# Finer first loads of Wq and later loads of bq and bk in a two-sublayer kernel (cross attention and quantised FFN)

## The reference

```python
def _L0_xattn_ref(text, features, Wq, bq, Wk, bk):
    Q = jnp.einsum('btx,dx->btd', text, Wq) + bq
    K = jnp.einsum('bpx,dx->bpd', features, Wk) + bk
    scores = jnp.einsum('btd,bpd->btp', Q, K) * scale
    attn = jax.nn.softmax(scores, axis=-1)
    return jnp.einsum('btp,bpd->btd', attn, features)

x = x + _L0_xattn_ref(_layernorm(x), ctx_4096, Wq, bq, Wk, bk)
x = x + _L0_ffn_ref(_layernorm(x), qweight, qzeros, scales, bias, g_idx)
```

## Time and profile before

| | before |
|---|---|
| median of three runs | 555.83 us |
| the profiled execution, its own time | 556.69 us |
| its span | 554.9 us |
| TensorE matmul busy | 546.3 us (98%) |
| VectorE busy | 385.4 us (69%) |
| ScalarE busy | 239.1 us (43%) |
| GpSimd busy | 186.1 us (34%) |
| first stage's share of the DMA: 0 to 16 us | 200 to 420 GB/s, engines nearly always busy |

### The profile page before, as it was taken

How to read it: one execution, slowest core, us unless ns; L and a number is a source line. 1 busy time by engine, 2 the same in 40 slices (tenths; PEclk the granted TensorE clock), 3 DMA queues, 4 the chain that set the end, 5 groups by cost and what they waited for, 6 DMA issues and landing times.

```text
span 554.9 us, 7445 instructions
## 1 busy us (share of the span) xinstructions
PE 546.3 (98%) x2702; PEld 456.5 (82%) x2702; DVE 385.4 (69%) x643; ACT 239.1 (43%) x426; POOL 186.1 (34%) x143
## 2 busy tenths in 40 slices
PE   7999999999999999999999999999999999999997
PEld 5888888887777877878889999999788888888886
DVE  4987776689889997784213555574877788778742
ACT  5964354301431341242427666676473253234210
POOL 2072000000000000000125977776667545743630
PEclk9999999999999999999999999999999999999999
DMA  8842100349677745743345699897517776773411
GB/s 270 275 156 73 38 1 0 112 160 314 207 205 262 220 190 175 220 168 143 130 138 203 250 350 351 318 402 301 229 77 227 229 219 235 214 241 108 123 76 76
DMA packets 47187, 106.59 MB, mean 192 GB/s; under 512 B 3576, under 2 KB 24064, under 8 KB 44976
## 3 DMA queue, kind: packets, MB, share of 16 engines
q1 hardware_dynamic: 40624, 99.84, 51.2%
q10 hardware_dynamic: 6528, 6.29, 5.2%
HBM read 66.27 MB, written 39.85 MB: 191 GB/s over the span
## 4 chain that ended last, share of the span: by engine, by line
PE 86%; DVE 5%; ACT 4%; DMA 2%; issue 2%; POOL 1%; SPq 0%; ACTq 0%; DVEq 0%; POOLq 0%
PE bank L1235 22%; PE bank L1237 22%; PE bank L1236 22%; PE bank L1279 5%; PE bank L1282 5%; PE bank L1285 5%; PE bank L1337 2%; DMA wk_stage<-in_L_xattn_Wk 1%; DMA right_scratch<-part_hi 1%; ACT yin L789 1%; POOL cn_lo L537 1%; PE bank L1245 1%; ACT cn_hi L586 1%; PE bank L1320 1%; DVE junk L1001 0%
## 5 line engine op out<-in xcount | busy, mean ns | idle before, releaser
L1235 PE MATMUL bank<-xT_hi,m_hi 128*128 128x512 f32 x256 | 103.4, 404 | 0.4 <-DVE xT_lo L853 0.4
L1236 PE MATMUL bank<-xT_lo,m_hi 128*128 128x512 f32 x256 | 99.7, 389 | 0.0
L1237 PE MATMUL bank<-xT_hi,m_lo 128*128 128x512 f32 x256 | 99.7, 389 | 0.0
L745 ACT ACTIVATE t_pair<-bank,ucol 128x512 f32<-128x512 f32 x32 | 22.0, 686 | 107.0 <-PE bank L1237 107.0
L544 POOL TENSOR_TENSOR tT_lo<-t_pair,tT_hi 128x1024 fp32r<-128x1024 f32 x16 | 38.2, 2405 | 75.0 <-ACT tT_hi L586 75.0
L1187 DVE TENSOR_TENSOR xres<-xres,bank 128x512 f32<-128x512 f32 x56 | 38.1, 681 | 36.2 <-PE bank L1237 36.1
L523 POOL TENSOR_TENSOR pairs<-mv,pairs 128x2 f32<-128x2 f32 x8 | 5.5, 692 | 161.3 <-DVE mv L920 161.3
L558 POOL TENSOR_TENSOR l_lo_s<-l_sum_s,l_hi_s 128x512 fp32r<-128x512 f32 x32 | 40.4, 1298 | 56.0 <-DVE l_sum_s L1128 56.0
L1235 PEld LDWEIGHTS bank<-xT_hi,m_hi 128*128 128x128 f32 x256 | 48.1, 188 | 12.3 <-DVE xT_lo L853 0.8
L1237 PEld LDWEIGHTS bank<-xT_hi,m_lo 128*128 128x128 f32 x256 | 48.0, 188 | 10.1
L1236 PEld LDWEIGHTS bank<-xT_lo,m_hi 128*128 128x128 f32 x256 | 48.1, 188 | 9.9 <-issue 0.2
(11 more groups left out here) (148 smaller groups left out, 1255.7 us busy)
## 6 DMA issues: line engine op xcount, KB each, us to landing
cin<-in_ctx SPq DMA_DIRECT2D x8, 1024.0 KB, 5.7
xres<-in_x SPq DMA_DIRECT2D x8, 1024.0 KB, 11.2
out<-xres SPq DMA_DIRECT2D x15, 512.0 KB, 5.7
right_scratch<-part_hi SPq DMA_DIRECT2D x28, 256.0 KB, 2.2
xn_scratch<-xin SPq DMA_DIRECT2D x6, 1024.0 KB, 4.9
xq<-xn_scratch ACTq DMA_DIRECT2D x24, 256.0 KB, 5.6
r_tile<-right_scratch SPq DMA_DIRECT2D x6, 1024.0 KB, 11.3
yn_scratch<-yin SPq DMA_DIRECT2D x6, 1024.0 KB, 4.4
```

The costliest lines, as they stand in the source:

```text
L745: act.activation(t_pair[p][:, :, j, :], bank[n % 4][:, :].rearrange("p (b q) -> p b q", b=2), ACT.Identity, bias=ucol[:, j:j + 1]).then_in ...
L1235: pe.matmul(out_, a_hi, b_hi, start=start, stop=False, skip_group_check=True)
L1236: pe.matmul(out_, a_hi, b_lo, start=False, stop=False, skip_group_check=True)
L1237: return pe.matmul(out_, a_lo, b_hi, start=False, stop=stop, skip_group_check=True)
```

## The change

Three edits, all in the first stage.

1. The first load of each of Wq's blocks 0 and 1 carries two K tiles (128 KB) and no longer four (256 KB). The K tiles 2 and 3 of both blocks are loaded behind slice 1 of Wk; tiles 4 to 7 stay where they were, behind slice 2. ScalarE and VectorE split the first two tiles alone (`first_split`), and tiles 2 and 3 in front of slice 2's split; TensorE waits for them at c = 2.
2. bq and bk are loaded behind slice 4 of Wk, where they stood in front of slice 2.
3. `times_bq` and `add_u` run two slices later: `times_bq(c - 4)` behind the split of slice c. Four of them are left for behind the loop, where two were.

```diff
+            def first_wq(b, lo, hi, done):
+                sp.dma_start(wq_stage[b][:, lo:hi, :], wq_rows[:, lo:hi, b * P:(b + 1) * P]).then_inc(done, 16)
-            first_wq(0, 0, s_wq0[0])
+            first_wq(0, 0, 2, s_wq00[0])
             for h, done in enumerate((s_wk0, s_wkl[0])):
                 cols = slice(h * HALF, (h + 1) * HALF)
                 sp.dma_start(wk_stage[0][:, cols], wk_rows[:, 0, cols]).then_inc(done, 16)
-            first_wq(1, 0, s_wq0[1])
+            first_wq(1, 0, 2, s_wq00[1])
             for c in range(1, NB):
                 if c == 2:
-                    for r, row in enumerate((bq, bk)):
-                        sp.dma_start(bcols[:, r, :], row.rearrange("(p c) -> p c", c=NB)).then_inc(s_small, 16)
+                    for b in range(2):
+                        first_wq(b, 2, KH, s_wq0[b])
                 if c == 3:
                     for b in range(2):
-                        first_wq(b, 1, s_wql[b])
+                        first_wq(b, KH, NB, s_wql[b])
...
                 sp.dma_start(wk_stage[c % N_STAGE], wk_rows[:, c, :]).then_inc(s_wkl[c % N_STAGE], 16)
+                if c == 4:
+                    for r, row in enumerate((bq, bk)):
+                        sp.dma_start(bcols[:, r, :], row.rearrange("(p c) -> p c", c=NB)).then_inc(s_small, 16)
...
         @block.scalar
+            def first_split(b):
+                act.wait_ge(s_wq00[b], 16)
+                copy(wq_hi[b][:, 0:2, :], wq_stage[b][:, 0:2, :]).then_inc(s_wqhi0, 1)
+
             def wq_split(b, h):
-                cs = slice(KH * h, KH * (h + 1))
+                cs = slice(2 if b < 2 and h == 0 else KH * h, KH * (h + 1))
...
+                if c == 2:
+                    wq_split(0, 0)
+                    wq_split(1, 0)
...
-                if c > 1:
-                    times_bq(c - 2)
-            times_bq(NB - 2)
-            times_bq(NB - 1)
+                if c > 3:
+                    times_bq(c - 4)
+            for c in range(NB - 4, NB):
+                times_bq(c)
...
         @block.vector
+            def first_split(b):
+                dve.wait_ge(s_wqhi0, b + 1)
+                low(wq_lo[b][:, 0:2, :], wq_stage[b][:, 0:2, :], wq_hi[b][:, 0:2, :], s_wqlo0)
...
-                if c > 2:
-                    add_u(c - 2)
-            add_u(NB - 2)
-            add_u(NB - 1)
+                if c > 4:
+                    add_u(c - 4)
+            for c in range(NB - 4, NB):
+                add_u(c)
...
         @block.tensor
+                if first:
+                    pe.wait_ge(s_wqhi0, 1)
+                    pe.wait_ge(s_wkhi, 1)
+                elif b == 1 and c == 0:
+                    pe.wait_ge(s_wqlo0, 2)
+                elif c == KH or c == (2 if b < 2 else 0):
+                    pe.wait_ge(s_wqlo, wq_split_count(b, c // KH))
```

More of the change, by code:

```diff
@@ L194, in xattn_ffn_kernel @@
         s_wk0 = sem("half_of_first_wk_slice_loaded")
+        s_wq00 = [sem(f"first_of_wq_block{i}_loaded") for i in range(2)]
         s_wq0 = [sem(f"half_of_wq_block{i}_loaded") for i in range(2)]
+        s_wqhi0, s_wqlo0 = sem("first_of_wq_hi"), sem("first_of_wq_lo")
         s_wkl = [sem(f"wk_loaded{i}") for i in range(N_STAGE)]
@@ L319, in load_wq @@
                 sp.dma_start(wq_stage[b % 3], wq_rows[:, :, b * P:(b + 1) * P]).then_inc(s_wql[b % 3], 16)
-            def first_wq(b, h, done):
-                cs = slice(KH * h, KH * (h + 1))
-                sp.dma_start(wq_stage[b][:, cs, :], wq_rows[:, cs, b * P:(b + 1) * P]).then_inc(done, 16)
-            first_wq(0, 0, s_wq0[0])
+            def first_wq(b, lo, hi, done):
+                sp.dma_start(wq_stage[b][:, lo:hi, :], wq_rows[:, lo:hi, b * P:(b + 1) * P]).then_inc(done, 16)
+            first_wq(0, 0, 2, s_wq00[0])
             for h, done in enumerate((s_wk0, s_wkl[0])):
@@ L611, in times_bk @@
                 ins.then_inc(s_wqbk, 1)
-            wq_split(0, 0)
+            first_split(0)
             for h, loaded in enumerate((s_wk0, s_wkl[0])):
@@ L617, in _ @@
                 copy(wk_hi[:, 0, cols], wk_stage[0][:, cols]).then_inc(s_wkhi, 1)
-            wq_split(1, 0)
+            first_split(1)
             for c in range(1, NB):
+                if c == 2:
+                    wq_split(0, 0)
+                    wq_split(1, 0)
                 if c == 3:
@@ L1283, in proj @@
                     if first:
-                        pe.wait_ge(s_wqlo, 1)
+                        pe.wait_ge(s_wqlo0, 1)
                     ins = pe.matmul(out_, q_lo, wk_hi[:, c, cols], start=False, stop=c == NB - 1, skip_group_check=True)
```

## The result

| | before | changed |
|---|---|---|
| median of six runs | 555.74 us | 559.57 us |
| lowest and highest | 555.34, 557.14 | 558.86, 559.94 |
| ratio of the changed kernel to the one before | | 1.0063, 95% interval 1.0052 to 1.0074 |
| span of the profiled execution | 554.9 us | 557.7 us |

The prediction was 555.4 us with a range of 554.4 to 556.6. The changed kernel is 3.5 us slower by the ratio (555.74 x 0.0063), and 3.8 us by the medians.

A forecast was written before the change was run, and what follows sets the result against it. TensorE was taken as the bound from end to end: 0.85 us gained at c = 1, 0.4 lost again in front of block 3, so 555.83 - 0.4 = 555.4 us, range 554.4 to 556.6.

The forecast's parts named there:

- Slice 1 was to land at 8.1: First stage's start: halved first loads bring Wk's slice 1 in 0.85 us earlier, 0.3 to 1.05.
- two more loads don't delay slice 2: Loads behind slice 1: slice 2 still lands at 10.67 at the latest, just in time for c = 2.
- Edit 2's price of 0 to 0.45 us for bq and bk: Between landings of slices 1 and 2: the small pieces of bq and bk cost this much, taken as 0.3 us.
- 1.7 us between slices 1 and 2: ScalarE's time there was to cover the splits of tiles 2 and 3, about 0.8 us, at no cost.
- The 0.17 us: DMA in front of slice 2: estimated cost of 256 packets of bq and bk over 16 engines at 10.5 ns each.
- SyncE's queue waited for the product: Refill of Wk's buffers: slice 6 is issued only after the later bq product, at 16.92 us, landing at 20.32.
- X = T + 17.28: VectorE's queue: end of block 3's first low part, counted from slice 7's landing with five additions; 40.8 us.
- T: Landing of Wk's slice 7: taken as 23.5 us against 21.21 before, bounds 22.8 and 24.7.
- C: Rival: late buffer refill makes block 3 wait, 0.76 us at T = 24.7, up to 556.6 us; chance 0.22.
- the prediction's own formula: Gain left at block 3's start is 23.94 - T, forecast 0.44 us.
- Rival B: Slice 7 lands before 23.1 us and the whole gain is kept: 555.0, down to 554.8 us; chance 0.15.
- Behind that the slack comes back: After block 3's start no more waits: later blocks have one low part and one sum each in 10.9 us of matmuls.

The follow-up runs named there:

- experiment 1: Changed kernel with bq, bk, their products and additions put back, so only the smaller first loads of Wq differ from the kernel before: ratio 0.9997.
- 3: Changed kernel with eight buffers for Wk's slices in place of six: 555.51 us, ratio 0.9993 to the kernel before.
- exp. 11: Kernel before with 8 warming transposes on TensorE in place of 24, a control: 555.83 us, ratio 0.9995.
- 4: Kernel before with eight buffers for Wk's slices in place of six, a control: 556.18 us, ratio 0.9997.
- 10: Changed kernel with 8 warming transposes on TensorE in place of 24 and nothing else: 557.83 us, ratio 1.0026 to the kernel before.
- experiment 9: Changed kernel with tables, packed weight and x waiting for slice 7's low part, and 8 warming transposes in place of 24: 555.89 us, ratio 0.9996.
- 2: Kernel before with bq and bk loaded behind slice 4 and products and additions two slices later, first loads unchanged: 559.64 us, ratio 1.0061.
- 5: Kernel before with only the bq and bk products and their additions two slices later: 559.83 us, ratio 1.0066.
- 6: Kernel before with slices 6 and 7 issued only when the high parts of slices 4 and 5 are made: 556.76 us, ratio 1.0005.
- 7: Changed kernel with tables, packed weight and x issued only after slice 7's low part is made: 558.47 us, ratio 1.0043 to the kernel before.
- experiment 8: Kernel before with slices 6 and 7 issued late, and tables, packed weight and x waiting for slice 7's low part: 555.99 us, ratio 0.9997.
- experiment 12: Kernel before with slices 6 and 7 issued late and only the seven small table loads waiting for slice 7's low part: 556.67 us, single execution.

## Why the prediction was wrong

**Edit 1: right in mechanism and size.** Slice 1 was to land at 8.1 and c = 1 to start at 10.5; measured 8.11 and 10.48. That two more loads don't delay slice 2 was right in the changed kernel (10.31) and wrong in experiment 1 (11.14), where bq and bk stood in front of it as well. Edit 2's price of 0 to 0.45 us for bq and bk can be neither confirmed nor refuted: the landings of slice 2 scatter by 0.8 us in either order. Two steps on the way were wrong without an effect. ScalarE did not have 1.7 us between slices 1 and 2 for the two splits: slice 1's own high part takes 1.06 of it, and 0.66 were idle; the splits took 0.70 in place of 0.8, and the slices came 2.20 us apart. That the gain reaches the total time isn't shown: the intervals of experiments 1 and 3 touch 1.

The 0.17 us that the prediction works out from the Trainium skill ("DMA: Bandwidth & Descriptors", Measured) is a wrong sum. The 10.5 ns stand there for a 4 KB transfer of 64 packets that takes 0.67 us in all, so the engines' working side by side is in them already, and as an estimate by them 256 packets come to 2.7 us. No run here shows that.

**Edit 3: the mechanism was right.** SyncE's queue waited for the product as said (slice 6 asked for at 16.7, landed 20.4), VectorE's queue was the path, and X = T + 17.28 was measured as T + 17.5. TensorE waited in front of block 3 for the low part of Wq named in the text. Also right: C, the direction of the loss.

**The step that failed is T, slice 7's landing.** "Block 2 follows 1.77 us later, and slice 7 1.27 to 1.80 us after it": I took 23.5 with bounds 22.8 and 24.7; it was 26.07, because 3.5 us passed between block 2 and slice 7. Put into the prediction's own formula, T = 26.07 gives 23.94 - 26.07, a loss of 2.1 us, and block 3 started 2.2 us late. The term that was mis-sized is this last one, 1.27 to 1.80 us. What it measures, from the last event of block 2 to the last of slice 7:

| | tables right behind slice 7 | tables made to wait |
|---|---|---|
| no fetch inside the transfer | 1.76 (before), 1.92 (exp. 11), 2.77 (4), 3.09 (3), 3.53 (1), 3.35 (10) | 1.24 (9) |
| fetch inside it | 3.54 (changed), 3.62 (2), 4.11 (5), 3.42 (6) | 2.85 (7), 1.24 (8) |

(With only the small tables made to wait and no fetch inside, experiment 12, it is 2.27.) So 1.2 us is what is left when nothing else is under way, and the 1.80 that I took for the upper end was a lucky reading of one profile: with the same order of the queue and with slice 7 asked for early, in experiments 1, 3 and 4, it was 2.8 to 3.5. Being late is therefore not what made the tables cost something; they already stood beside slice 7 in the kernel before. Rival B says so ("may have shared the engines with it") and then sets them aside, since they "come the same way". What being late did bring is the fetch: it lies inside slice 7's transfer in every profile with a late slice 7 and 24 warming transposes except that of experiment 12, and in none with an early one. It was in the page of the profile (the row `q8 instruction: 21, 0.34, 0.3%`), and the prediction doesn't ask when it runs. With T = 23.66 (experiment 9) the same formula gives 23.94 - 23.66 = 0.3 us of gain, and the ratio measured there is 0.9996: the forecast, under the condition that it assumed, though the interval (0.9987 to 1.0006) can't tell a gain of 0.3 us from none.

**A smaller miss:** "Behind that the slack comes back". TensorE stopped once more, at the first matmul of block 3's second half (49.49, due at about 49.2), behind a low part that took 2.03 us and not 0.7. The prediction had counted one low part for each later block, and a block has two, one for each half of its K tiles. The last section has the 2.03.

**What stays open.** The medians differ by 3.5 to 3.8 us, the two profiled executions by 2.8; the kernel before varies by 1.8 us from run to run, and its profiled execution was one of the slower. Which share of the landing belongs to the tables and which to the fetch in an average run isn't settled: the four ratios above aren't additive, and there is one profile of each. Nor is it known why, by the table above, the tables cost 0.5 us in one profile and 2.3 in another with the same order behind slice 7, or the fetch nothing in experiment 8 and 1.6 in 7. In the changed kernel's profile three engines were late, and the fetch, one packet on one engine, was over at 22.3 us; the tables should have the larger part there, by argument alone.

## What to carry to other kernels

A product that frees a load buffer is part of the load queue: if it moves, price the landing of everything behind that buffer, and look for what else will be on the DMA engines at the new time, instruction fetches among it. A load has landed when the last of its sixteen events is there (26.07 for slice 7, where the thirteenth came at 24.31), so one late engine is enough to delay it. The spacing of two landings in one profile is one draw: the same spacing was 1.8 to 3.5 us here, and a bound should come from several profiles or hold at least one disturbance. Slack that two things draw on (here a later landing and two more additions behind it) can be spent only once: each alone was nearly free, both together cost 3.5 us.

## What the hardware showed beyond that

- One VectorE subtraction of 128 x 512 with both inputs in SBUF took 2.03 us in place of 0.69 to 0.71, while GpSimd ran a subtraction of its own:

```profile
46.74 2.15 POOL L520 TENSOR_TENSOR sc_f<-sc_f,s 8x1024 f32<-8x1024 f32 x1
...
47.41 2.03 DVE L864 TENSOR_TENSOR wq_lo<-wq_stage,wq_hi 128x512 fp32r<-128x512 f32 x1
```

  It ends 0.55 us after GpSimd's instruction. In the kernel before it is the same instruction that took 1.48 us, and it also ended 0.55 us after GpSimd's subtraction (43.24, 43.79). So it is in all fourteen profiles: it starts 0.7 to 1.2 us into GpSimd's instruction, takes 1.48 to 2.04 us, and ends 0.54 to 0.56 us behind it. That the one holds the other is still an inference; no run here takes GpSimd's instruction away. The Trainium skill ("SBUF — State Buffer", its section on the two separate sides) has a rule that would explain it: a VectorE operation with two SBUF inputs and a GpSimd operation that reads SBUF take turns at a shared pair of ports, and the one that comes second is held for the other's whole instruction. The traces agree in that the end follows GpSimd's; the 0.55 us left are a little less than the 0.70 that the subtraction takes by itself.
- Slice 6 took 3.7 us from issue to landing in a queue that had run empty (experiments 6 and 7); a slice behind others lands 1.27 us after them.
- With 8 warming transposes in place of 24 the first products of TensorE took 0.63 to 0.80 us each where they take 0.39 to 0.51, one every 0.43 us and not 0.23, up to 10.6 us in experiment 9 and 12.9 in 11. The granted clock of these stretches reads 1.00 in the profiles with 8 and with 24, so the rows don't name the reason. The median was no higher (0.9995), though in the profiled execution of the control c = 1 started at 11.62 and block 3 at 42.26, 0.3 and 0.9 us later than before.
